# Expert output bias beside the weights and added on DVE; result rows added by scatters into two output regions

## The reference

```python
x = x + xattn(layernorm(x), ctx, ctx, ...)
# ffn on xf = layernorm(x), 2048 tokens
logits = xf @ Wg                       # 16 experts, top 2
gates = softmax(where(mask, logits, -inf))
y = 0
for e in range(16):
    h = silu(xf @ W1[e] + b1[e]) * (xf @ W11[e] + b11[e])      # 128 -> 256
    y = y + (h @ W2[e] + b2[e]) * gates[:, e, None]            # 256 -> 128
z = silu(xf @ Ws1 + bs1) * (xf @ Ws11 + bs11) @ Ws2 + bs2
return x + (y + z)
```

## Time and profile before

| | us |
|---|---|
| median of 3 runs | 338.8 |
| lowest and highest | 338.71, 342.55 |
| profiled execution | 339.4 |
| its span, first to last instruction | 337.6 |
| PE busy, share of the span | 281.9, 84% |
| DVE busy | 215.7, 64% |
| POOL busy | 124.4, 37% |

### The profile page before, as it was taken

The page is one execution under the profiler, slowest core; times in us unless marked ns, Lnnn a source line. Parts: engine busy times, 40 slices in busy tenths (PEclk is TensorE's granted clock), DMA queues, the critical chain, the costliest instruction groups (busy, mean ns, idle before and its releaser), DMA issues.

```text
span 337.6 us, 6077 instructions
## 1 busy us (share of the span) xinstructions
PE 281.9 (84%) x1869; PEld 207.5 (61%) x1869; DVE 215.7 (64%) x712; ACT 161.9 (48%) x317; POOL 124.4 (37%) x203
## 2 busy tenths in 40 slices
PE   0138799899999899998998988988899999999900
PEld 0026455465656456565564556877789999999900
DVE  7976945575574777758677368864445565555606
ACT  1413555555595454954558556452344544544400
POOL 0324023223311332565318300537106666666630
PEclk9999999999999999999999999999999999999965
DMA  7999500000000000000000100114616858484237
GB/s 267 344 374 398 238 2 0 1 2 2 2 0 0 2 0 3 25 26 8 8 2 33 34 0 1 34 34 123 193 32 175 254 151 249 139 248 132 74 109 289
DMA packets 21759, 33.80 MB, mean 100 GB/s; under 512 B 2672, under 2 KB 11600, under 8 KB 21600
## 3 DMA queue, kind: packets, MB, share of 16 engines
q1 hardware_dynamic: 19200, 28.20, 26.3%
q0 software_dynamic: 2528, 5.22, 4.5%
HBM read 23.95 MB, written 9.45 MB: 99 GB/s over the span
## 4 chain that ended last, share of the span: by engine, by line
PE 66%; DVE 18%; ACT 5%; issue 4%; DMA 4%; SPq 1%; POOL 1%; POOLq 0%; DVEq 0%; ACTq 0%
PE ps L1383 7%; PE ps L1365 6%; DVE mpad L576 6%; PE ps L1371 6%; PE ps L1295 5%; PE ps L1109 4%; PE ps L1138 4%; PE ps L1152 4%; PE ps L1069 4%; PE ps L1070 4%; PE ps L1071 4%; PE ps L1110 3%; PE ps L1148 3%; PE ps L1122 3%; PE ps L1136 3%
## 5 line engine op out<-in xcount | busy, mean ns | idle before, releaser
L576 DVE TENSOR_REDUCE mpad<-ps 128x2 f32<-128x308 f32 x128 | 55.3, 472 | 36.4 <-PE ps L1110 36.0
L818 POOL TENSOR_SCALAR ks<-k_stack,cst 128x160 fp32r<-128x160 f32 x64 | 30.0, 483 | 100.1 <-DVE k_stack L561 100.1
L890 POOL DMA_INDIRECT result_rows<-yo,dest x47 | 45.1, 960 | 41.4 <-DVE yo L792 41.1
L955 ACT ACTIVATE pf<-ps 128x512 f32<-128x512 f32 x80 | 46.5, 597 | 18.2 <-PE ps L1152 10.2
L1110 PE MATMUL ps<-ks,qs 96*128 96x308 f32 x128 | 46.2, 416 | 0.0
L856 POOL DMA_INDIRECT slot_rows<-xr,slot x32 | 31.3, 979 | 37.3 <-DVE slot L483 28.8
L1109 PE MATMUL ps<-mq_b,identb 128*128 128x308 bf16 x128 | 38.8, 308 | 4.8 <-DVE mpad L576 3.8
L1138 PE MATMUL ps<-qs,ks 128*128 128x512 f32 x64 | 37.1, 581 | 0.0
L1109 PEld LDWEIGHTS ps<-mq_b,identb 128*128 128x128 bf16 x128 | 12.5, 98 | 33.0 <-issue 26.3
L783 DVE SCALAR_TENSOR_TENSOR e_h<-ps,wu,e_s 128x128 f32<-128x128 f32 x62 | 19.0, 347 | 20.0 <-PE ps L1371 19.9
L1056 ACT ACTIVATE e_s<-ps,wu 128x128 f32<-128x128 f32 x62 | 19.4, 364 | 25.1 <-PE ps L1365 25.1
(11 more groups left out here) (203 smaller groups left out, 628.5 us busy)
## 6 DMA issues: line engine op xcount, KB each, us to landing
wu<-w_up SPq DMA_DIRECT2D x31, 258.0 KB, 3.3
wr<-w_up SPq DMA_DIRECT2D x1, 4128.0 KB, 22.2
slot_rows<-zero SPq DMA_DIRECT2D x1, 3120.0 KB, 24.5
xg<-slot_rows SPq DMA_DIRECT2D x12, 260.0 KB, 3.4
wd<-w_down SPq DMA_DIRECT2D x1, 2048.0 KB, 12.1
xo<-result_rows SPq DMA_DIRECT2D x4, 512.0 KB, 5.4
xs<-x SPq DMA_DIRECT2D x1, 1024.0 KB, 4.8
out<-xs SPq DMA_DIRECT2D x4, 256.0 KB, 2.3
```

Source lines behind the costliest of these rows:

```text
L576: dve.tensor_reduce(mpad[:, m % 2, q, 96 + 2 * a:98 + 2 * a], ps[:, KS_ + a, 0:2 * SK].rearrange("p (c k) -> p c k", c=2), AX.X, ALU.max, ...
L890: pool.indirect_dma_start(out=result_dram[:, :], out_offset=bass.IndirectOffsetOnAxis(ap=dest[:, n:n + 1], axis=0), in_=yo[:, n % 4, :], i ...
L955: act.activation(pf[:, n % RP, :], ps[:, ST_ + n % 2, :], ACT.Exp, scale=DK ** -0.5).then_inc(exp_done, 1)
```

## The change

The bias b2[e] is laid out 128 times beside the up weights of its expert in DRAM (`w_up`: 644 columns for 516), so that it comes with `wr` and `wu`. `result` adds it on DVE to the PSUM sum, into `y_b`, and then multiplies `y_b` by the gate. `bias_step`, `b_all`, `tile_one` and the bias product on PE are gone. The ring has RW = 8 slots for 6, and a slot is free at `yo_done` instead of `eh_done`, since the bias in it is read last.

`out` is now three regions of rows: 512 spare rows, 2048 first rows, 2048 second rows. SP writes zeros to the spare rows, bs2 to the second rows and, as each batch of `xs` is complete, `xs` to the first rows (`store_first`). Each scatter adds its rows to `out`: first picks to the first region, second picks to the second. At the end POOL issues one DMA that adds the second region to the first in DRAM. The pair loads, the DVE adds behind the loop and the final stores are gone.

```diff
-RW = 6
+RW = 8
-WU = 2 * H + 4
+WB = 2 * H + 4
+WU = WB + D
 @@ sync
+            sp.wait_ge(ld_b, 16)
             sp.wait_ge(cleared, 1)
...
+            sp.dma_start(out[0:SPARE, :].rearrange("(p a) d -> p (a d)", p=P), zero[:, 0:4 * D]).then_inc(primed, 16)
+            sp.dma_start(second_rows, bsr[:, :].unsqueeze(1).to_broadcast([P, NT, D])).then_inc(primed, 16)
...
+            def store_first(c):
+                sp.wait_ge(x2_done, c + 1)
+                sp.dma_start(first_rows[:, QT * c:QT * c + QT, :], xs[:, QT * c:QT * c + QT, :]).then_inc(primed, 16)
...
                 if d >= RW:
-                    sp.wait_ge(eh_done, 2 * (ring[d - RW] + 1))
+                    sp.wait_ge(yo_done, ring[d - RW] + 1)
...
             for d in range(RW):
                 load_weights(d)
+            for c in range(2):
+                store_first(c)
             sp.wait_ge(sent, 2 * NT * 16)
             for g in range(2):
                 load_rows(g)
+            for c in range(2, B):
+                store_first(c)
...
-            for r in range(4):
-                sp.wait_ge(returned[r], (RUN - r + 3) // 4 * 16)
-            pairs = result_dram[SLOTS:SLOTS + 2 * TOK, :].rearrange("(p t k) d -> p t k d", t=NT, k=2)
-            for c in range(B):
-                sp.dma_start(xo[:, QT * c:QT * c + QT, :, :], pairs[:, QT * c:QT * c + QT, :, :]).then_inc(ld_r[c], 16)
-            for c in range(B):
-                sp.wait_ge(out_done, c + 1)
-                sp.dma_start(out[:, QT * c:QT * c + QT, :], xs[:, QT * c:QT * c + QT, :]).then_inc(stored, 16)
 @@ vector, result(n)
-                dve.tensor_scalar(yo[:, n % 4, :], ps[:, Y_ + n % 2, 0:D], gate[:, n:n + 1], None,
+                dve.tensor_tensor(y_b[:, n % 2, :], ps[:, Y_ + n % 2, 0:D], up_weights(n)[:, WB:WB + D],
+                                  ALU.add).then_inc(y_summed, 1)
+                dve.wait_ge(y_summed, n + 1)
+                dve.tensor_scalar(yo[:, n % 4, :], y_b[:, n % 2, :], gate[:, n:n + 1], None,
                                   ALU.mult).then_inc(yo_done, 1)
 @@ gpsimd
+            pool.wait_ge(primed, 16 * (2 + B))
             for n in range(RUN):
                 pool.wait_ge(yo_done, n + 1)
-                pool.indirect_dma_start(out=result_dram[:, :],
+                pool.indirect_dma_start(out=out[:, :],
                                         out_offset=bass.IndirectOffsetOnAxis(ap=dest[:, n:n + 1], axis=0),
-                                        in_=yo[:, n % 4, :], in_offset=None).then_inc(returned[n % 4], 16)
+                                        in_=yo[:, n % 4, :], in_offset=None, compute_op=ALU.add
+                                        ).then_inc(returned[n % 4], 16)
+            for r in range(4):
+                pool.wait_ge(returned[r], (RUN - r + 3) // 4 * 16)
+            pool.dma_start(out[SPARE:SPARE + TOK, :].rearrange("(p t) d -> p (t d)", p=P),
+                           out[SPARE + TOK:SPARE + 2 * TOK, :].rearrange("(p t) d -> p (t d)", p=P),
+                           accum_op=ALU.add, max_dma_last_dim=4096).then_inc(stored, 16)
 @@ tensor, down(n, e)
-                pe.matmul(o, tile_one[:, block_of(n):block_of(n) + 1].to_broadcast([P, P]), b_all[:, :], start=True, stop=False)
                 for c in range(2):
```

More of the change, by code:

```diff
@@ L42 @@
 RUN = TILES - 1
+SPARE = 4 * P
 GROUPS = (0, 4, 5, 1, 6, 7, 2, 8, 9, 3, 10, 11)
@@ L163, in build @@
         wr = sb("wr", [P, NE, WU])
-        b_raw = sb("b_raw", [NB, D])
-        b_part, b_sel = (sb(n, [NB, D], BF16) for n in ("b_part", "b_sel"))
-        b_all = sb("b_all", [P, D], BF16)
+        y_b = sb("y_b", [P, 2, D])
         attention = ExitStack()
@@ L209, in build @@
         te = sb("te", [1, TILES], I32)
-        tile_one = sb("tile_one", [P, TILES], BF16)
         xg = sb("xg", [P, 2, 4, XW])
@@ L235, in build @@
          q_part_done, qs_done, smax_mm, max_done, mt_mm, qmax_done, st_mm, exp_done, pv_mm, os_done, ot_mm,
-         on_done, ont_mm, ont_done, x1_mm, x1_done, w_split, b_step, lg_done, ex_in, ex_done, copied, sel_done,
+         on_done, ont_mm, ont_done, x1_mm, x1_done, w_split, lg_done, ex_in, ex_done, copied, sel_done,
          rank_mm, rank_read, slots_done, sent, tile_known, te_summed, te_mm, a_mm, b_mm, silu_done, h_done, w2_mm,
          x2_done, tx_mm, xgt_done, meta_done, gate_mm, lin_mm, esilu_done, eh_done,
-         ey_mm, yo_done, out_done, stored, ld_d) = (sem(n) for n in (
+         ey_mm, yo_done, stored, primed, y_summed, ld_d) = (sem(n) for n in (
             "ld_x ld_c ld_w ld_m ld_ctx ld_b zeroed dve_step cleared scanned "
@@ L250, in build @@
         ld_u = [sem(f"ld_u{r}") for r in range(RW)]
-        ld_r = [sem(f"ld_r{c}") for c in range(B)]
         returned = [sem(f"returned{r}") for r in range(4)]
@@ L258, in up_weights @@
             return wr[:, e, :] if e < NE else wu[:, rung(n) % RW, :]
+        first_rows = out[SPARE:SPARE + TOK, :].rearrange("(p t) d -> p t d", p=P)
+        second_rows = out[SPARE + TOK:SPARE + 2 * TOK, :].rearrange("(p t) d -> p t d", p=P)
         block = stack.enter_context(nc.Block())
@@ L675, in batch @@
                         batch_norm(b, -1)
-                    if b == 0 and g in (1, 2):
-                        if g == 1:
-                            dve.wait_ge(ld_b, 32)
-                            link(dve.tensor_tensor(b_raw[:, :], b_raw[:, :], bsr[:, :], ALU.add))
-                        for k in range(5 * g - 5, 5 * g):
-                            bias_step(k)
             norm_block(2)
@@ L723, in publish_tiles @@
                 dve.wait_ge(te_mm, 1)
-                dve.tensor_scalar(tile_one[:, :], ps[:, M_, 0:TILES], cst[:, C_WHO:C_WHO + 1], None, ALU.is_equal)
                 dve.tensor_copy(te[:, :], ps[0:1, M_, 0:TILES]).then_inc(tile_known, 1)
@@ L802, in _ @@
                     meta(n // 4 + 1)
-            for c in range(B):
-                dve.wait_ge(ld_r[c], 16)
-                rows = xs[:, QT * c:QT * c + QT, :]
-                link(dve.tensor_tensor(rows, rows, xo[:, QT * c:QT * c + QT, 0, :], ALU.add))
-                dve.tensor_tensor(rows, rows, xo[:, QT * c:QT * c + QT, 1, :], ALU.add).then_inc(out_done, 1)
         @block.gpsimd
@@ L1425, in constants @@
     c[:, C_TILE:C_TILE + TILES] = np.arange(TILES)
-    c[:, C_SPARE:C_SPARE + TILES] = P * np.arange(TILES) + p[:, None]
+    c[:, C_SPARE:C_SPARE + 4] = P * np.arange(4) + p[:, None]
     for k in range(2):
-        c[:, C_DEST + NT * k:C_DEST + NT * k + NT] = SLOTS + 2 * (NT * p[:, None] + np.arange(NT)) + k
-    for r in range(3):
-        c[:, C_PART + r] = p // NE == r
+        c[:, C_DEST + NT * k:C_DEST + NT * k + NT] = SPARE + TOK * k + NT * p[:, None] + np.arange(NT)
     c[:, C_ROW] = p
-    c[:, C_WHO] = np.where(p < NB, p % NE, -1)
     return c
@@ L1469 @@
     biases = np.concatenate([np.asarray(v).reshape(NE, 2, P) for v in (L0_ffn_b1, L0_ffn_b11)], axis=1).transpose(0, 2, 1)
+    b2 = np.tile(np.asarray(L0_ffn_b2).reshape(NE, 1, D), (1, P, 1))
     arrays = {
@@ L1494 @@
            for name, a in arrays.items()]
-    out = nc.dram_tensor("out", (P, NT, D), F32, kind="ExternalOutput").ap()
+    out = nc.dram_tensor("out", (SPARE + 2 * TOK, D), F32, kind="ExternalOutput").ap()
     build(nc, *aps, out)
     r = run_bass_kernel_spmd(nc, [arrays], core_ids=[0])
-    return r.results[0]["out"].transpose(1, 0, 2).reshape(B, S, D)
+    rows = r.results[0]["out"][SPARE:SPARE + TOK].reshape(P, NT, D)
+    return rows.transpose(1, 0, 2).reshape(B, S, D)
```

46 lines of the change are left out of this document (12 added, 34 removed).

## The result

| | before | after |
|---|---|---|
| median of the timed runs, us | 338.75 (4 runs) | 371.63 (4 runs, 370.57 to 372.22) |
| profiled execution: span, us | 337.6 | 369.5 |
| ratio of the times, 95% interval | | 1.094 [1.086, 1.103] |

The changed kernel is 9.4% slower, 32.9 us; the forecast was 12 us more than before.

What follows compares the result with a forecast made beforehand. TensorE was taken to bound the expert loop. On the profiled 339.4 us, -2.0 (`bias_step`), +16.8 (SP queue), -1.2 (bias products) and -1.6 (tail) gave 351.4; the median, 0.6 lower, was forecast at 350.8, range 343.5 to 362.

Steps and rivals of the forecast that it cites:

- the mechanism of the queue: SP queue in the expert loop: row loads stand behind weights now released by `yo_done`, stopping TensorE; +16.8 us.
- `bias_step` and the products ahead of the transposes at 254.33: Before that point: `bias_step` gone from two first-batch attention steps, and three bias products gone; -2.3 us.
- nine intervals: Expert loop, between transposes of successive groups: 72.9 us where 56.1 stood, from late row loads; +16.8.
- from the last transposes to the issue of the last scatter: End of the expert loop, after the last group's transposes until POOL issues its last scatter; -0.6 us.
- from there to the end: From the last scatter's issue to the kernel's end, with one adding DRAM-to-DRAM DMA as tail; -1.9 us.
- the eight places named: Transposes where TensorE waits for late rows in the expert loop: 2.9 us six times, some 1.6 twice.
- I take POOL's time unchanged: Scatters in the expert loop: POOL's 0.96 us each kept; even twice that covered by 2.18 per tile.
- Rival C: Adding scatters bind the expert loop: POOL needs 2.22 us a tile, +14, 365 us; chance 0.07.
- Q: SP's queue in the expert loop: rows stand behind weights whose release is now `yo_done`; forecast +16.8 us.
- POOL's new wait on `primed` costs 0: Entry of the expert loop: the last of four stores lands by the first scatter at 252.46; 0 us.
- The 41 us of idle time: POOL's idle time in the expert loop, said to let it catch up if its first scatter started late.
- End 0.2: Last term of the tail, after the final DRAM-to-DRAM DMA has landed: 0.2 us to the kernel's end.

Runs made afterwards that it cites:

- plain_scatter_2: Changed kernel with scatters that overwrite instead of adding, so the output lacks that sum: 360.88 us, 1.058 of the kernel before.
- plain_early_2: Changed kernel with scatters that don't add and each group's rows issued two steps earlier on SP's queue: 338.81 us, 0.997 of the kernel before.
- rows_early_2: Changed kernel, scatters still adding, with each group's rows issued two steps earlier on SP's queue: 357.76 us, 1.055 of the kernel before.
- plain_filled: Changed kernel with scatters that don't add and 24 extra TensorE transposes before the waits for rows of groups 3 to 10: 361.00 us, 1.060.
- before_add_scatter: Kernel before with scatters that add, into result rows zeroed early by one more DMA: 355.53 us, 1.044 of the kernel before.
- before_late_release_2: Kernel before with 8 weight slots, released at `yo_done` instead of `eh_done`: 355.80 us, 1.040 of the kernel before.

## Why the prediction was wrong, step by step

It said 350.8, in 343.5 to 362; it was 371.6. The sign and the mechanism of the queue held, the size did not. By spans, +31.9 was measured and +12.0 forecast. The 19.9 between them are: 9.1 for the lower clock behind the stops, for which there was no term; 5.8 for POOL's time, taken as unchanged, at the end of the loop; 2.6 in the tail; 1.4 for a first scatter that came late; and 1.2 for rows that landed later than assumed, less 0.2.

| term | forecast | measured |
|---|---|---|
| `bias_step` and the products ahead of the transposes at 254.33 | -2.3 | -2.2 |
| nine intervals | +16.8 | +28.2 |
| from the last transposes to the issue of the last scatter | -0.6 | +5.2 |
| from there to the end | -1.9 | +0.7 |

The first `mpad` reductions, in the timeline of DVE, to be set beside the earlier trace rows:

```profile
47.35 0.86 DVE L574 TENSOR_REDUCE mpad<-ps 128x2 f32<-128x308 f32 x2 [2.54 <-PE ps L1088]
...
56.39 0.86 DVE L574 TENSOR_REDUCE mpad<-ps 128x2 f32<-128x308 f32 x2 [2.00 <-PE ps L1088]
...
65.41 0.86 DVE L574 TENSOR_REDUCE mpad<-ps 128x2 f32<-128x308 f32 x2 [1.99 <-PE ps L1088]
...
75.02 0.86 DVE L574 TENSOR_REDUCE mpad<-ps 128x2 f32<-128x308 f32 x2 [2.00 <-PE ps L1088]
```

and the one that follows the second half of `bias_step`, in the kernel before:

```profile
77.28 0.86 DVE L576 TENSOR_REDUCE mpad<-ps 128x2 f32<-128x308 f32 x2 [2.00 <-PE ps L1110]
```

**The first row of the table is right by luck.** The step with the first half of `bias_step` fell from 10.04 to 9.02, as said. The one with the second half fell from 9.99 to 9.61 only, 0.4 us for the 1.0 that was taken over to it. The other 0.9 came before 48.23, where this trace starts its steps at 47.35, ahead of any `bias_step`. That start lies anywhere from 46.8 to 51.4 in the profiled executions of all these kernels, also in kernels that are the same up to there, so it is no gain of the change.

**Right.** The queue of SP holds TensorE at the eight places named; from transposes to rows it is 4.73 and 4.72 us in the intervals at the full clock (predicted 4.87); rows take 3.26 to 4.83, mean 3.95, for the 3.8 assumed, +1.2 in all. DVE's pair `y_b`, `yo` starts 0.31 apart and takes 0.6, for 0.67 assumed: covered.

**One failed step is "I take POOL's time unchanged".** An adding scatter takes 1.56 + 0.30 us of POOL. The prediction checked 1.92 + 0.30 against the mean of 2.18 per tile and called it covered but for the edge. But the results don't come at their mean. Behind a stop they come in bunches, 1.34 apart within a bunch, where POOL needs 1.87 for each. Before the next stop has ended it has worked the bunch off: behind each of the stops of 2.6 to 4.1 us the next scatter follows its `yo` after 0.28 us again. So up to the last stop the mean did cover it. The last twelve tiles have no stop. That shows as the 5.8 us by which the third row of the table passed its forecast: twelve scatters back to back, the first at 333.62 and the last at 354.22. From the last transposes to the last scatter it is 12.3 us with plain scatters, for 17.8 (plain_scatter_2, 332.39 to 344.71). Rival C was this mechanism, with 1.92 for 1.56; it lacked that the two delays overlap, as the table of four shows. Taken for itself the adding scatter costs 15 to 19 us; in the changed kernel, beside Q, leaving it out gives back some 11. The prediction also gave 6.8 us as the longest landing of a plain scatter; that view takes in the loads of the pairs, and the longest landing of a scatter was 4.9. Nothing in its sum rests on it.

**"POOL's new wait on `primed` costs 0" held, but the first scatter is late all the same.** Timeline of POOL and DVE at the entry:

```profile
250.31 0.29 DVE L770 TENSOR_SCALAR yo<-y_b,gate 128x128 f32<-128x128 f32 x1
...
253.66 1.62 POOL L862 DMA_INDIRECT out<-yo,dest  x1 [18.59 <-DVE yo L770]
...
257.17 0.29 DVE L767 TENSOR_TENSOR y_b<-ps,wu 128x128 f32<-128x128 f32 x1 [1.37 <-DMA out<-yo,dest]
```

`yo` is ready at 250.60 and the scatter comes 3.06 us later; before it came 0.28 us behind its `yo`. It isn't the wait for the stores: the last of the four was issued at 245.03 and had landed 2.3 us later. The view of the transfers from 250.5 to 253.5, in 40 slices, has one packet:

```profile
DMA  0000000000000000400000000000000000000000
...
q14 instruction: 1, 0.01, 1.0%
```

It is a load of instructions at 251.7, 1.1 us behind `yo` and 2 us ahead of the scatter. plain_scatter_2, plain_early_2 and rows_early_2 have such a packet and the same delay (`yo` at 249.55, 253.40 and 250.68, scatter at 252.51, 256.47 and 253.69), and so has plain_filled; the kernel before has neither. Behind it a `yo` slot is returned late, DVE's `y_b` waits 1.37 us for it, the weights are released late, and the rows of the first interval go out at T + 6.27 (plain_scatter_2: T + 6.50) instead of T + 4.87. That POOL waited for its own instructions is what this points to; no run took the load away, so it is not shown. The Trainium skill (Runtime: NRT & Kernel Launch, "Instruction fetch mechanics") calls the cost of passing from one block of instructions to the next mostly hidden. Here 3 us would not be, on an engine that had just waited; since it is not shown that this load was POOL's, no run here contradicts the page. The 41 us of idle time that were to absorb a late start belonged to scatters of 0.96 us.

**The other failed step, and the larger: the clock was put at nothing.** The prediction priced every step at the full clock, and a stop as its own length. Five of the intervals that begin at the lower clock, after stops of 2.6 to 4.1 us, issue the rows at T + 6.98, 4.80, 6.36, 4.90 and 6.36 for the forecast 4.87, 3.53, 4.87, 3.53 and 4.87: 7.7 us together, and the last interval adds 1.4 for the same reason. With the 1.4 of the first interval, the 1.2 of the landings, and 0.3 that two intervals gained, this is the 11.4 us by which the nine intervals passed the forecast. plain_filled shows the cause: at the full clock all the later issues come as forecast. The Trainium skill (TensorE: Matmul & The Clock Gate, "HAM oscillation — how this bites in real kernels") describes a kernel whose bursts of products between waits for transfers each restart at the lower clock. The traces agree in that, with longer bursts and stops of 2.6 to 4.1 us, and the prediction should have priced it. In the second interval of the changed kernel DVE had waited for returned scatters as well, but its last wait ended at 262.36, before the transposes at 262.60, and the products behind them start 0.85 apart until 267.53; so the T + 6.98 is the clock's. The lower clock also took up part of the two short stops: they are 0.74 and 0.86 us for the 1.6 forecast.

**The tail** was to gain 1.9 from the issue of the last scatter on, and lost 0.7. The landing of the last scatter grew by 1.0 as taken (3.27 for 2.26), POOL woke 0.7 after it instead of 0.13, and from the issue of the last DMA at 358.20 to the end it is 11.3 us, for 9.2. The DMA itself was quicker than taken, landing after 7.7 us for 9.0. The term that failed is "End 0.2": from the landing at 365.9 to 369.5 it is 3.6 us. POOL's closing instruction fills them (the view of L125, start and duration):

```profile
L125 POOLq DRAIN  x1: 11097/11097/11097, 358.2 to 358.2; - x1
```

It starts at 358.17, beside the last DMA, and ends at 369.27, 3.3 us behind the landing. plain_scatter_2 has 11192 ns from 347.64 and the same 3.3 us behind its landing at 355.51. In the kernel before POOL's closing instruction had ended at 330.5, and SP's last store was followed by the end after 0.5 us. No run has the last DMA issued another way, so that this length comes of POOL having issued it is argued and not shown. With plain scatters the new tail is 14.4 us (plain_scatter_2, 344.71 to 359.1) for 14.6 before. The trade of loads, DVE adds and stores for one adding DMA gives nothing on this kernel.

## What to carry over

An engine that has time to spare on the average may still be the bound where its work comes in bunches; set the new duration against the spacing within each stretch, the last one above all, and not against the mean. A buffer's release should be judged by what stands behind its wait in the same queue: here it moved back by 3.6 us (from the end of `e_h` of tile 4 at 254.74 to that of its result at 258.34, in the kernel before), which the weights had to spare, and it stopped TensorE for up to 4 us, since the next group's rows were behind them. And a stop of TensorE costs more than its length.

## What the runs showed of the hardware

- An indirect scatter of 128 rows of 512 bytes that adds holds POOL 1.55 to 1.56 us for 0.96. It lands in 3.8 to 4.3 us by the median and never under 3.2 (the changed kernel, before_add_scatter, rows_early_2), where plain ones land in 3.1 to 3.7 by the median and 2.2 at the least (the kernel before, before_late_release_2, plain_filled, plain_scatter_2). The add is not only a matter of the second read: by the Trainium skill (Collectives: The Full Stack, "Why ReduceScatter is half of AllGather") an adding transfer pays for its two reads, and that says nothing of the 0.60 us which here fall on the engine that issues it.
- TensorE restarted at 1.2 GHz behind each stop of 2.55 to 4.06 us in the changed kernel, plain_scatter_2 and before_late_release_2, 0.85 us for four products instead of 0.45, for 3.8 us of work in the rows shown and 4.9 behind the longest stop of the changed kernel. Stops of 1.28, 2.20 and 2.42 us in plain_scatter_2 were followed by 0.45, as those of 0.74 and 0.86 were in the changed kernel.
- The first scatter came 3.0 to 3.1 us behind its data in the five kernels whose traces show a load of instructions in between, and 0.28 us behind it in the kernel before. That the load is the cause is not shown.
- A 1 MB adding DMA from DRAM to DRAM landed 7.7 us after its issue, which itself took POOL 0.98 us, and POOL's closing DRAIN ended 3.3 us behind that landing, in the changed kernel and in plain_scatter_2.
